# An audio tower on one core: the score matmul pairs of the attention are issued twice

## The reference, cut to what matters

```python
scores = q @ k.T          # (750, 16) x (16, 750) -> 750 x 750
p = exp(scores - max)     # the maximum over the keys of a row
out = (p / p.sum()) @ v   # (750, 750) x (750, 16)
```

## Time and profile before

| | |
|---|---|
| median of 3 runs | 3766.42 us (3764.93, 3766.42, 10893.9) |
| the profiled execution | 3744.26 us, span of its trace 3742.4 us |
| PE busy, matmuls | 3436.9 us, 92% |
| PE weight loads | 1743.4 us, 47% |
| DVE busy | 2123.1 us, 57% |
| ACT busy | 1690.9 us, 45% |
| POOL busy | 532.2 us, 14% |
| mean granted TensorE clock | 0.782 of 2.4 GHz |
| matmul records of a score form | 2304 of A, 2304 of B |
| chain that ended last | PE 74%, DVE 10%, ACT 5% |

### The profile page before, as it was taken

One profiled execution on the slowest core, in us unless ns is written; L12 is line 12 of the kernel. 1 busy time (PEld: TensorE's weight loads), 2 busy tenths in 40 slices (PEclk: granted clock), 3 DMA queues, 4 the chain that ended last, 5 costly groups with the idle time before them and its releaser, 6 DMA issues.

```text
span 3742.4 us, 55987 instructions
## 1 busy us (share of the span) xinstructions
PE 3436.9 (92%) x22512; PEld 1743.4 (47%) x22512; DVE 2123.1 (57%) x3793; ACT 1690.9 (45%) x2291; POOL 532.2 (14%) x1033
## 2 busy tenths in 40 slices
PE   6889999999999999999999999999999999999987
PEld 3443354443535445353544535344354544545455
DVE  3346474746656465664646566464665646566645
ACT  1115454636354353544435354453635445364642
POOL 1401020203011020300203020020301102020201
PEclk9876596976968687695867868587796858778899
DMA  5331101101010110101011010100101011020000
GB/s 119 106 98 53 43 24 45 28 26 46 17 51 16 45 28 13 53 24 42 25 41 32 13 53 18 48 22 30 46 14 53 15 45 28 7 61 10 18 7 7
DMA packets 121058, 137.35 MB, mean 37 GB/s; under 512 B 29505, under 2 KB 109722, under 8 KB 118798
## 3 DMA queue, kind: packets, MB, share of 16 engines
q1 hardware_dynamic: 118620, 126.22, 11.5%
q0 software_dynamic: 1280, 7.08, 0.8%
q10 hardware_dynamic: 898, 0.47, 0.1%
HBM read 77.84 MB, written 55.30 MB: 36 GB/s over the span
## 4 chain that ended last, share of the span: by engine, by line
PE 74%; DVE 10%; ACT 5%; issue 2%; POOL 1%; DVEq 0%; ACTq 0%; POOLq 0%
PE ps L1114 70%; DVE negp L925 6%; ACT big L730 3%; PE ps L1201 2%; PE ps L1290 1%; DVE parts L920 1%; ACT hn L695 1%; DVE st L869 1%; DVE rest L1029 0%; PE ps L1246 0%; DVE h0t L1057 0%; ACT x2Ah L683 0%; ACT xA L681 0%; PE ps L1404 0%; PE ps L1269 0%
## 5 line engine op out<-in xcount | busy, mean ns | idle before, releaser
L925 DVE TENSOR_REDUCE negp<-ps 125x2 f32<-125x750 f32 x1152 | 1062.6, 935 | 922.6 <-PE ps L1114 919.9
L730 ACT ACTIVATE big<-ps,wsc 125x750 f32<-125x750 f32 x1152 | 1012.8, 887 | 827.5 <-PE ps L1114 824.1
L1114 PE MATMUL ps<-big,V 125*32 125x188 f32 (+1 forms) x9216 | 783.7, 432 | 13.1 <-issue 11.2
L1114 PE MATMUL ps<-qs,ks 50*125 50x375 f16 x2304 | 550.4, 475 | 84.3 <-DVE negp L925 81.8
L1114 PE MATMUL ps<-ks,qs 48*125 48x375 f16 x2304 | 526.8, 455 | 105.3 <-DVE parts L920 47.9
L1029 DVE SCALAR_TENSOR_TENSOR rest<-ps,fb,h1s 128x375 f32<-128x375 f32 (+1 forms) x448 | 251.7, 603 | 347.0 <-PE ps L1114 345.7
L1114 PEld LDWEIGHTS ps<-qs,ks 50*125 50x125 f16 x2304 | 184.3, 157 | 566.3 <-issue 351.4
L498 POOL TENSOR_TENSOR h0t<-h0t,onrm 125x384 f32<-125x384 f32 x48 | 48.1, 1003 | 2496.2 <-DVE onrm L956 2496.2
L1114 PEld LDWEIGHTS ps<-big,V 125*32 125x32 f32 x9216 | 223.4, 125 | 366.8 <-issue 349.6
L745 ACT ACTIVATE h1s<-ps,fb,wsc 128x375 f32<-128x375 f32 (+1 forms) x448 | 272.5, 659 | 228.6 <-PE ps L1114 228.6
L1114 PEld LDWEIGHTS ps<-ks,qs 48*125 48x125 f16 x2304 | 198.6, 170 | 318.6 <-issue 117.3
(11 more groups left out here) (185 smaller groups left out, 3382.4 us busy)
## 6 DMA issues: line engine op xcount, KB each, us to landing
v_scratch<-vtmp SPq DMA_DIRECT2D x16, 1125.0 KB
V<-v_scratch SPq DMA_DIRECT2D x48, 375.0 KB
ks<-qk_scratch SPq DMA_DIRECT2D x288, 46.9 KB, 2.0
qs<-qk_scratch SPq DMA_DIRECT2D x288, 46.9 KB, 2.0
qk_scratch<-parts SPq DMA_DIRECT2D x32, 375.0 KB, 3.7
h_scratch<-h0t SPq DMA_DIRECT2D x16, 562.5 KB
hn<-h_scratch SPq DMA_DIRECT2D x16, 562.5 KB
h0t<-h_scratch SPq DMA_DIRECT2D x16, 562.5 KB
```

The costliest lines, as they stand in the source:

```text
L730: nc.scalar.activation(probs[:, i % 2, 2 * c:2 * c + 2, HC * n:HC * n + HC], slot(s, TP), ACT.Exp, scale=wsc[0:TP, 21:22]).then_inc(exp_do ...
L925: V_.tensor_reduce(negp[:, 2 * n:2 * n + 2], slot(s, TP), axis=AX.X, op=MAX, negate=True).then_inc(max_done, 1)
L1114: return nc.tensor.matmul(o, l, r, start=start, stop=stop)
```

## The change

A constant is added, and the loops over the two matmuls of an A tile and of a B tile run over (0, 1, 0, 1) in place of (0, 1). So each tile has four matmuls: q = 0, q = 1, and then the same two again with the same operands, into the same PSUM banks, each starting its result anew (`start=True`), so that the second pair writes the same values over the first. Only the last of the four raises `a_done` or `b_done`. Nothing else is changed.

```diff
@@ -42,6 +42,7 @@
 HP = HG // 2
+WARM_A, WARM_B = 2, 2
 MSCALE = 32768.0
@@ -1249,7 +1250,7 @@
             def a_tile(g, n, s):
 
                 c, j, n2 = n // (2 * J), n % (2 * J) // 2, n % 2
-                for q in range(2):
+                for q in WARM_A * (0, 1):
                     r = slice(64 * q, 64 * q + KROWS)
                     ins = mm(slot(s, TP)[:, q, :], qs[r, g, NF * c + TP * j:NF * c + TP * j + TP],
                              ks[r, g, NF * c + HC * n2:NF * c + HC * n2 + HC])
@@ -1258,7 +1259,7 @@
             def b_tile(g, k, s):
 
                 i, n, c = k // HG, k % HG // HP, k % HP
-                for q in range(2):
+                for q in WARM_B * (0, 1):
                     r = slice(64 * q, 64 * q + KROWS + MROWS)
                     ins = mm(slot(s, TP)[:, q, :], ks[r, g, NF * c + TP * i:NF * c + TP * i + TP],
                              qs[r, g, NF * c + HC * n:NF * c + HC * n + HC])
```

## The result

The changed kernel takes **3443.62 us** (median of 4 runs, 3428.83 to 3450.98) against 3765.68 for the kernel before: ratio 0.9147, 95% interval 0.9117 to 0.9177. The forecast was 3450, in a range from 3340 to 3860. A ratio leaves out runs over 1.5% longer than the fastest of the same kernel; here that is one of the kernel before, of 10893.9 us.

A forecast was written before the change was run, and what follows sets the result against it. PE was taken as the bound, slowed by its clock. Eleven sequences at -22 us (-242), two together -28, first and last two bodies -42 gave -312: 3432 profiled, plus 22 for the median, 3450 us; range 3340 to 3860.

The forecast's parts named there:

- Two speeds of the same work: Score tile cycles run stably at 1.2 or 2.4 GHz; a whole sequence takes 221.9 us at 0.76, 211.6 at 0.81.
- The price of a pair, 0.16 us: In each A or B tile, a second pair was taken to add 0.16 us at full clock.
- The rival without overlap: In each tile the second pair starts when the first ends, costing 0.37 us, not 0.16: 3885 us, chance 0.07.
- the assumed 0.31: Cost in us of a second pair in a score tile at 1.2 GHz, taken as twice the full-clock price.
- The cycle of 1.24 us: PE's doubled cycle of B, A and V part at full clock: 0.92 + 2 x 0.16 = 1.24 us.
- The sum: Whole kernel: -22 us in each of eleven sequences, less in the others, -312 in total.
- Why falls come: Waits of PE at full clock precede falls; second pairs fill roughly a third of them, so most falls don't come.
- the prediction's three falls: Clock falls after stretches at 1568.4, 1455.6 and 1442.0 us, with PE waiting 1.0 to 1.6 of 3.3 to 3.5 us.
- The rule against it: A busy PE is granted full rate, so second pairs buy nothing where PE has no idle time and are all cost.
- the first rival: In the slow cycle the clock keeps its pattern and doubled tiles cost 28.5 us a sequence: 4180 us, chance 0.15.
- The rival on the slower side: The clock stays at 1.2 GHz until the same transposes and products as before: 4180 us, chance 0.15.
- the rival of half and half: Clock falls at the projections, stays low to the output transposes, then high; +3.5 us a sequence, 3815 us, chance 0.20.

The follow-up runs named there:

- A alone: Only the A tiles are issued twice, the B tiles once, where the changed kernel doubles both: 3659.92 us, ratio 0.9603 to the kernel before.
- B alone: Only the B tiles are issued twice, the A tiles once, where the changed kernel doubles both: 3450.71 us, ratio 0.9175 to the kernel before.
- e11: Against the changed kernel, both kinds doubled only among the projections, in the first body and before it, 28 of 144 tiles a sequence: 3401.69 us, ratio 0.9041.
- the pair of 16 rows: Changed kernel with each tile's first pair multiplying only 16 rows of each half instead of 48 or 50: 5116.15 us, ratio 1.3574 to the kernel before.

## Why the prediction was right, point by point

**Two speeds of the same work.** Right: 0.76 to 1.00 in a sequence, slow stretches gone. That the clock is the cause is shown from three sides: a third pair at full clock only costs (+236 us); the order of times follows the mean clock in the runs with equal work (A alone against B alone); and with the third section uncovered the slow stretch is back where it was. That it is the order of issue or the later release everywhere is excluded by e11, which has the whole gain with 116 of 144 tiles issued as before. With the pair of 16 rows the order was that of the changed kernel, and the clock fell all the same.

**The price of a pair, 0.16 us.** Right, and in the same banks as well: 0.37 from doubled tile to doubled tile for 0.21 before. The rival without overlap is out. So is the Trainium skill's rule (TensorE: Matmul & The Clock Gate, Part 3) as a stop for this case: a load is recorded with 0.13 us and a score matmul with over 0.3, so 0.16 us leaves no room for a load that waits until its own row group has finished. At half clock the assumed 0.31 holds too: with all but the third section doubled, an A tile is followed by a V part after 0.50 us where it is single (1919.95 to 1920.45) and after 0.82 where it is doubled (1933.56 to 1934.38).

**The cycle of 1.24 us.** Right to the hundredth.

**The sum.** -22 us a sequence was forecast, -23.9 measured (221.9 to 198.0), with three sequences of 200 to 201 that have a short fall. The total in the profiled executions: 3744.3 - 3447.2 = 297 for 312. Counted from the start of one feed-forward layer to the next, the eleven sequences from 707.7 to 3145.4 us of the trace before gained 253 us for 242, and all that surrounds them 44 for 70. What was mis-sized is that rest: from the last feed-forward layer to the end it took 204.5 us before and 207.3 after, nothing gained. That the median came within 7 us of 3450 is in part luck: the 22 us added for the distance of the median from the profiled execution was -4 after, which more than made up for the 15 us too many in the sum. The waits were put at 6 us in what had been slow; a whole late sequence now has 12.1 us of idle PE (198.0 - 185.9) against 13.8.

**Why falls come.** The mechanism was half wrong. The prediction had PE's waits as what precedes a fall and filling them as what prevents it. At the end of the second section this fits: where PE was idle for 1.18 of 3.30 us before the fall at 1571.7, it is now idle for 0.75 of 10.00:

```profile
1655.00:1665.00 10.00, 9.25 (x122) 4.55 (x120) 9.79 (x27) 6.62 (x8) 8.88 (x22) 1.00 0.11 32
```

But the wait behind a projection is still there. The changed kernel's stretch that answers to 1455.6 to 1459.1 of the earlier trace rows, and the tile after the wait:

```profile
1566.00:1569.50 3.50, 2.54 (x32) 0.89 (x28) 2.55 (x3) 1.53 (x2) 0.00 (x0) 1.00 0.00 0
```

```profile
1568.16 0.53 PE L1115 MATMUL ps<-ks,qs 48*125 48x375 f16 x4 [0.96 <-DVE parts L921]
```

The 65 us of half clock began behind a fourth stretch, which the prediction's three falls leave out. Here it is before, with the tile after its wait, and then the tile that answers to it in the changed kernel:

```profile
1472.80:1476.20 3.40, 2.28 (x17) 0.75 (x15) 1.78 (x2) 1.68 (x2) 0.00 (x0) 1.00 0.00 0
```

```profile
1475.91 0.37 PE L1114 MATMUL ps<-ks,qs 48*125 48x375 f16 x2 [1.12 <-DVE parts L920]
```

```profile
1581.15 0.53 PE L1115 MATMUL ps<-ks,qs 48*125 48x375 f16 x4 [0.96 <-DVE parts L921]
```

In both places PE waits 0.96 us for 1.12 before, in the first it is busy 2.54 us of 3.50 against 2.38, and the clock stays. Nor does waiting alone bring a fall: the early sequence of the earlier trace rows is idle for 4.1 of 31.7 us and stays at 1.00. With the pair of 16 rows PE was busy 97% and the clock fell. So among the projections it is hardly the idle time bought down, 0.16 us, that keeps the clock; what these stretches have more is the second pairs. Why they keep it is not shown. The place was right (the projections), and covering that place alone gives the gain.

**The rule against it.** The Trainium skill's rule (TensorE: Matmul & The Clock Gate, Part 1), that the gate follows how busy PE has been, would have given 4180 by the first rival. The runs here disagree with it as far as busy time is what the profile's rows call so: 20.40 of 20.40 us at 0.50, 97% at 0.65, and 92% both at 0.782 before and at 0.977 after. Whether another measure of being busy would fit no run here shows.

**The rival on the slower side** (clock unchanged, 4180) did not come. Nor did the rival of half and half come in the changed kernel. Its pattern came in the kernel that leaves the third section single: 3715 us, where the rival has 3815 with the third section doubled. Without its 11.5 us for doubled tiles before 1518 the rival's sequence would be 213.9 us; 218.4 was measured.

## What to carry to other kernels

Read the granted clock stretch by stretch before you trust "PE is the bound": here a mean of 0.782 means that 44% of the span, (1 - 0.782) x 2, ran at half clock, most of it with PE shown busy. If the same tiles run at both speeds in one trace and a fall lasts until other work ends it, as here, a few matmuls that are thrown away, put where the fall begins, can pay many times over: 28 pairs, 4.5 us of issue at 0.16 each, took a sequence from 221.9 us to between 190 and 202. Put everywhere they cost their issue time. Try the place by experiment, since small shifts decide whether a fall comes.

## What the runs showed of the hardware

- Matmuls of zeros kept the clock as real ones did (3438 against 3444 us, clock 0.97 and 0.98).
- PE busy 97% of the span at a clock of 0.65, with 16 rows in half of the score matmuls.
- Alternating 16-row and 50-row matmuls cost 1.01 us a tile of four at half clock, against 0.62 to 0.68 with equal rows. The Trainium skill, TensorEngine Tiling (Array Packing), Key Properties, says that a change of the tiling mode drains the engine; these rows agree if going from 16 to 50 rows is such a change, which no row tells.
- One repeated pair on the same rows and banks costs 0.16 us at full clock and 0.32 at half.
